# Attention scores in four 64x64 tiles, with the second token tile mirrored

## The reference, cut to what matters

```python
q = _l2norm(q) * q_scale
k = _l2norm(k) * k_scale
sim = jnp.einsum('bhid,bhjd->bhij', q, k) * ATTN_SCALE
dist = -jnp.abs(cols[None, :] - (rows[:, None] + NUM_NULL_KV))
sim = sim + dist[None, None] * slopes[None, :, None, None]
causal_mask = cols[None, :] > rows[:, None] + NUM_NULL_KV
sim = jnp.where(causal_mask[None, None], neg, sim)
attn = jax.nn.softmax(sim, axis=-1)
out = jnp.einsum('bhij,bhjd->bhid', attn, v)
```

## Time and profile before

| | us |
|---|---|
| median of 3 runs | 927.98 (927.37 to 929.27) |
| span of the profiled execution | 927.0 |
| PE busy | 867.1 (94%) |
| DVE busy | 765.1 (83%) |
| ACT busy | 585.8 (63%) |
| POOL busy | 562.4 (61%) |

### The profile page before, as it was taken

How to read it: one execution, slowest core, us unless ns; L and a number is a source line. 1 busy time by engine, 2 the same in 40 slices (tenths; PEclk the granted TensorE clock), 3 DMA queues, 4 the chain that set the end, 5 groups by cost and what they waited for, 6 DMA issues and landing times.

```text
span 927.0 us, 21283 instructions
## 1 busy us (share of the span) xinstructions
PE 867.1 (94%) x8062; PEld 689.6 (74%) x8062; DVE 765.1 (83%) x2457; ACT 585.8 (63%) x1255; POOL 562.4 (61%) x503
## 2 busy tenths in 40 slices
PE   0898899999999999999999999999999999999886
PEld 0685678688777878788787878678787878778676
DVE  6787799889898899889998899888998688865577
ACT  4518773967658672966648673866838774786631
POOL 5227763586638764586746865487644864467723
PEclk9989999999999999999999999999999999999999
DMA  6400000000000000000000000000000000000000
GB/s 165 113 1 0 13 2 2 1 12 2 14 1 0 13 2 13 1 13 1 14 1 1 13 2 14 0 13 2 2 13 1 1 13 2 1 1 1 3 12 12
DMA packets 21991, 11.46 MB, mean 12 GB/s; under 512 B 7552, under 2 KB 21248, under 8 KB 21760
## 3 DMA queue, kind: packets, MB, share of 16 engines
q1 hardware_dynamic: 20032, 9.50, 3.7%
q10 hardware_dynamic: 1856, 0.59, 0.3%
HBM read 7.99 MB, written 2.10 MB: 11 GB/s over the span
## 4 chain that ended last, share of the span: by engine, by line
PE 68%; DVE 16%; ACT 11%; issue 3%; POOL 1%; DMA 0%; SPq 0%; DVEq 0%; ACTq 0%; POOLq 0%
PE bank L1771 9%; PE bank L1772 8%; PE bank L1773 8%; PE bank L1784 5%; PE bank L2029 5%; PE bank L2086 4%; PE bank L1937 4%; PE bank L2035 3%; PE bank L2212 2%; PE bank L2218 2%; PE bank L2101 2%; PE bank L2076 2%; PE bank L2088 2%; PE bank L2187 2%; PE bank L2079 1%
## 5 line engine op out<-in xcount | busy, mean ns | idle before, releaser
L938 POOL TENSOR_TENSOR rnorm<-sumsq,minus_half 128x16 f32<-128x16 f32 x32 | 93.9, 2946 | 55.2 <-DVE sumsq L1574 55.2
L2029 PE MATMUL bank<-qT,kT 64*128 64x256 f32 x512 | 97.3, 387 | 0.0
L944 POOL TENSOR_TENSOR rnorm<-unit,minus_half 128x16 f32<-128x16 f32 x32 | 93.9, 2939 | 4.2 <-DVE unit L1580 4.2
L2035 PE MATMUL bank<-qT,kT 64*128 64x128 f32 x512 | 84.0, 284 | 5.1 <-ACT unit L1208 2.7
L1202 ACT ACTIVATE square<-bank,bias_k,rnorm 128x256 f32<-128x256 f32 x128 | 65.6, 570 | 35.8 <-PE bank L2029 35.8
L2035 PEld LDWEIGHTS bank<-qT,kT 64*128 64x128 f32 x512 | 71.0, 186 | 18.7 <-issue 5.7
L952 POOL TENSOR_SCALAR_AFFINE_SELECT square<-square 128x512 f32<-128x512 f32 x64 | 45.0, 704 | 61.6 <-ACT square L1208 61.5
L1132 ACT ACTIVATE xaT_hi<-bank 128x256 fp32r<-128x256 f32 x16 | 5.9, 382 | 111.1 <-PE bank L1945 110.7
L2029 PEld LDWEIGHTS bank<-qT,kT 64*128 64x128 f32 x512 | 68.7, 186 | 0.2
L2101 PE MATMUL bank<-w_out,qT 128*128 128x128 f32 x512 | 62.8, 276 | 1.2 <-DVE qT L1623 1.2
L1202 ACT ACTIVATE unit<-bank,bias_k,rnorm 128x256 f32<-128x256 f32 x96 | 51.4, 574 | 17.5 <-PE bank L2029 17.5
(11 more groups left out here) (419 smaller groups left out, 2902.7 us busy)
## 6 DMA issues: line engine op xcount, KB each, us to landing
xin<-in_L_attn_x SPq DMA_DIRECT2D x7, 256.0 KB, 2.8
out<-x SPq DMA_DIRECT2D x7, 256.0 KB, 2.3
square<-in_L_attn_w_kv SPq DMA_DIRECT2D x1, 1024.0 KB, 6.5
unit<-in_L_attn_w_q SPq DMA_DIRECT2D x1, 512.0 KB, 5.1
w_out<-in_L_attn_w_out SPq DMA_DIRECT2D x8, 64.0 KB, 2.1
xin<-in_L_attn_x ACTq DMA_DIRECT2D x1, 256.0 KB, 3.1
unit<-in_L_ffn_experts_gate ACTq DMA_DIRECT2D x1, 256.0 KB, 3.4
unit<-in_L_ffn_experts_up SPq DMA_DIRECT2D x1, 256.0 KB, 2.9
```

What stands on the lines that cost most here:

```text
L938: pool.tensor_tensor(rnorm[:, 1, t, :], sumsq[:, t % 2, :], minus_half[:], ALU.pow).then_inc(a_root.sem, 1)
L944: pool.tensor_tensor(rnorm[:, 0, ts, hs], k_sumsq[:, ts, hs], minus_half[:, hs].unsqueeze(1).to_broadcast([P, 2, H // 2]), ALU.pow).then_i ...
L2029: return mm(bank[s][:, 2 * P * i:2 * P * (i + 1)], kT[rs, p, 2 * P * b:2 * P * b + P], qT[rs, p, 2 * P * b:2 * P * (b + 1)], start=True, s ...
L2035: return mm(bank[2][:, 2 * P * s + P * i:2 * P * s + P * (i + 1)], kT[rs, p, ts], qT[rs, p, ts], start=True, stop=True)
```

## The change

Scores come in blocks of 64 keys, in tiles of 64 rows by 64 columns of the array, and each block streams only the queries that can see it: the early tile's first 64 keys 256 queries and its second 64 keys 192, the late tile's blocks 64 and 128. For the latter the late token tile of each sequence is mirrored (token 255 first): `l_x` and `a_nT_` turn odd tiles with a reversed identity. Then, in the late tile, a query sees the keys at its own place and behind it. The mask becomes two selections for each head pair, one for the early diagonal and one for the late with the comparison reversed. The weighted sums read the late queries backwards, so that the output is in token order; for this the matmul over 256 queries is split into two of 128. There are eight signals a unit from the scores instead of three, and the bias of the late keys counts from the other end.

```diff
@@ s_slopes (POOL)
-                for i, start in enumerate((-MID, -(MID + P), -(P - 1), 1)):
-                    made_by(pool.iota(zraw[:, i:i + 1], pattern=[[0, 1]], base=start, channel_multiplier=1, ...
+                for i, (start, step) in enumerate(((-MID, 1), (-(MID + P), 1), (-(P - 1), 1), (P, -1), (P - 1 - MID, -1))):
+                    made_by(pool.iota(zraw[:, i:i + 1], pattern=[[0, 1]], base=start, channel_multiplier=step, ...
@@ mask (POOL)
-                    pd = probs[h % 4][:, 0:4, :]
-                    pool.affine_select(out=pd, in_=pd, compare_op=ALU.is_ge, fill=0.0, base=0,
-                                       pattern=[[0, 4], [1, P]], channel_multiplier=-1).then_inc(a_mask.sem, 1)
-                pool.wait_ge(a_mask.sem, a_mask.at(g, 2 * c + 2))
+                    for step, tile in ((1, 0), (-1, 1)):
+                        pd = probs[h % 4][:, tile:4:2, :]
+                        pool.affine_select(out=pd, in_=pd, compare_op=ALU.is_ge, fill=0.0, base=0,
+                                           pattern=[[0, 2], [step, P]], channel_multiplier=-step).then_inc(a_mask.sem, 1)
+                pool.wait_ge(a_mask.sem, a_mask.at(g, 4 * c + 4))
@@ score_exps (ACT)
-                    act.wait_ge(a_s.sem, a_s.at(g, m + 1))
+                    act.wait_ge(a_s.sem, a_s.at(g, 6 * c + (6 if s else 2)))
...
-                    act.wait_ge(a_s.sem, a_s.at(g, 2 * c + 2))
+                    act.wait_ge(a_s.sem, a_s.at(g, 6 * c + 6))
@@ l_x, a_nT_ (PE)
+            def mirror_odd(dst, ts, src):
+                for t in ts:
+                    last = nc.tensor.transpose(dst[:, t * P:(t + 1) * P], src(t), ident[:, ::-1] if t % 2 else ident[:])
+                return last
@@ a_scores (PE)
-                key1(1, 0)
-                key0(0, 0)
-                key1(1, 1).then_inc(a_odd1.sem, 1)
-                key0(0, 1).then_inc(a_s.sem, 1)
-                key0(1, 0)
-                pe.wait_ge(a_odd1.sem, a_odd1.at(g, c + 1))
-                key1(0, 0)
-                key0(1, 1)
-                key1(0, 1).then_inc(a_s.sem, 1)
+                def early_keys(s, i, k):
+                    rs, cs, (p, b), n = slice(64 * s, 64 * s + 64), slice(64 * k, 64 * k + 64), part(i), 2 * P - 64 * k
+                    return mm(bank[s][cs, 2 * P * (i + 1) - n:2 * P * (i + 1)], kT[rs, p, 2 * P * b + 64 * k:2 * P * b + 64 * k + 64],
+                              qT[rs, p, 2 * P * (b + 1) - n:2 * P * (b + 1)], start=True, stop=True)
+                def late_keys(s, i, k):
+                    rs, cs, (p, b), n = slice(64 * s, 64 * s + 64), slice(64 * k, 64 * k + 64), part(i), 64 * k + 64
+                    tile1 = 2 * P * b + P
+                    return mm(bank[2][cs, 2 * P * s + P * i:2 * P * s + P * i + n], kT[rs, p, tile1 + 64 * k:tile1 + 64 * k + 64],
+                              qT[rs, p, tile1:tile1 + n], start=True, stop=True)
+                late_keys(1, 0, 1)
+                late_keys(1, 0, 0)
+                early_keys(0, 0, 0)
+                early_keys(0, 0, 1)
+                late_keys(1, 1, 0).then_inc(a_odd1.sem, 1)
+                late_keys(1, 1, 1).then_inc(a_odd1.sem, 1)
+                early_keys(1, 0, 0)
+                early_keys(0, 1, 1).then_inc(a_s.sem, 1)
+                early_keys(0, 1, 0).then_inc(a_s.sem, 1)
+                early_keys(1, 0, 1)
+                pe.wait_ge(a_odd1.sem, a_odd1.at(g, 2 * c + 2))
+                late_keys(0, 0, 1)
+                early_keys(1, 1, 0).then_inc(a_s.sem, 1)
+                early_keys(1, 1, 1).then_inc(a_s.sem, 1)
+                late_keys(0, 0, 0)
+                late_keys(0, 1, 1).then_inc(a_s.sem, 1)
+                late_keys(0, 1, 0).then_inc(a_s.sem, 1)
@@ a_mix_ (PE)
-                    last = mm(den[rs, P:2 * P], ones[:], late_sum[c % 2][:, i % 2, j, :], ...
+                    last = mm(den[rs, P:2 * P], ones[:], late_sum[c % 2][:, i % 2, j, ::-1], ...
...
-                        mm(parts[f][rs, :], val[:, 2 * b, h, fs], early(pr, j), start=True, stop=False, ...
+                        mm(parts[f][rs, 0:P], val[:, 2 * b, h, fs], early(pr, j)[:, 0, :], start=True, stop=True, ...
                     for rs, h, pr, j in quad:
-                        last = mm(parts[f][rs, P:2 * P], val[:, 2 * b + 1, h, fs], late(pr, j), start=False, stop=True, ...
+                        mm(parts[f][rs, P:2 * P], val[:, 2 * b, h, fs], early(pr, j)[:, 1, ::-1], start=True, stop=False, ...
+                    for rs, h, pr, j in quad:
+                        last = mm(parts[f][rs, P:2 * P], val[:, 2 * b + 1, h, fs], late(pr, j)[:, ::-1], start=False, stop=True, ...
```

More of the change, by code:

```diff
@@ L469, in program @@
         sel_f = qT[0:LOW + E0, 5, :]
-        zraw = sb("zraw", [P, 4])
+        zraw = sb("zraw", [P, 5])
         x0_loaded = sem("x0_loaded")
@@ L572, in program @@
         a_unit = signal("a_unit", T)
-        a_s = signal("a_s", H)
-        a_odd1 = signal("a_odd1", H // 2)
+        a_s = signal("a_s", 6 * U)
+        a_odd1 = signal("a_odd1", 2 * U)
         a_exp = signal("a_exp", 2 * H)
-        a_mask = signal("a_mask", H)
+        a_mask = signal("a_mask", 2 * H)
         a_late = signal("a_late", U)
@@ L695, in program @@
         POOL_SEL = POOL_IDENT + 7
-        POOL_SLOPE = POOL_SEL + 6 + H
+        POOL_SLOPE = POOL_SEL + 7 + H
         POOL_FILLED = POOL_SLOPE + 8
@@ L857, in s_slopes @@
                 made_by(pool.iota(par_i[:], pattern=[[0, 2]], base=0, channel_multiplier=1))
-                for i, start in enumerate((-MID, -(MID + P), -(P - 1), 1)):
-                    made_by(pool.iota(zraw[:, i:i + 1], pattern=[[0, 1]], base=start, channel_multiplier=1, allow_small_or_imprecise_dtypes=True))
+                for i, (start, step) in enumerate(((-MID, 1), (-(MID + P), 1), (-(P - 1), 1), (P, -1), (P - 1 - MID, -1))):
+                    made_by(pool.iota(zraw[:, i:i + 1], pattern=[[0, 1]], base=start, channel_multiplier=step, allow_small_or_imprecise_dtypes=True))
                 for h in range(H):
@@ L1044, in s_alibi @@
                 for dst, hs, i in ((bias_k0[:, 0:STEEP], slice(0, STEEP), 0), (bias_k0b[:], slice(0, STEEP), 1),
-                                   (bias_k1[:, 0:STEEP], slice(0, STEEP), 0), (bias_k0[:, STEEP:H], slice(STEEP, H), 2),
+                                   (bias_k1[:, 0:STEEP], slice(0, STEEP), 4), (bias_k0[:, STEEP:H], slice(STEEP, H), 2),
                                    (bias_k1[:, STEEP:H], slice(STEEP, H), 3)):
@@ L1946, in half_turn @@
                 return last
+            def mirror_odd(dst, ts, src):
+                for t in ts:
+                    last = nc.tensor.transpose(dst[:, t * P:(t + 1) * P], src(t), ident[:, ::-1] if t % 2 else ident[:])
+                return last
             def l_x(g, h):
                 pe.wait_ge(n_a.steps[h].sem, n_a.steps[h].at(g))
-                half_turn(down_bank(g, h), h, xa).then_inc(l_xt.sem, 1)
+                mirror_odd(down_bank(g, h), tiles(h), lambda t: xa[:, t, :]).then_inc(l_xt.sem, 1)
             def a_null(g):
@@ L2025, in part @@
                     return 2 * (c % 4) + i, seq
[L2027 to L2036, removed]
@@ L2053, in a_nT_ @@
                     pe.wait_ge(l_pick.sem, l_pick.at(g + 1, 1))
-                turn(bank[3], lambda t: null_p[:, t, :, :].rearrange("p i r -> p (i r)")).then_inc(a_nT.sem, 1)
+                mirror_odd(bank[3], range(T), lambda t: null_p[:, t, :, :].rearrange("p i r -> p (i r)")).then_inc(a_nT.sem, 1)
             def a_mix_(g, c):
@@ L2058, in a_mix_ @@
                 quad = [(slice(32 * i, 32 * i + 32), QW * q + i, probs[(2 * c + i % 2) % 4], i // 2) for i in range(QW)]
-                pe.wait_ge(a_mask.sem, a_mask.at(g, 2 * c + 2))
+                pe.wait_ge(a_mask.sem, a_mask.at(g, 4 * c + 4))
                 if c:
@@ L2078, in a_mix_ @@
                 for i, (rs, h, pr, j) in enumerate(quad):
-                    last = mm(den[rs, P:2 * P], ones[:], late_sum[c % 2][:, i % 2, j, :], start=True, stop=True, skip_group_check=True)
+                    last = mm(den[rs, P:2 * P], ones[:], late_sum[c % 2][:, i % 2, j, ::-1], start=True, stop=True, skip_group_check=True)
                 last.then_inc(a_den.sem, 1)
@@ L2085, in a_mix_ @@
                     for rs, h, pr, j in quad:
-                        mm(parts[f][rs, :], val[:, 2 * b, h, fs], early(pr, j), start=True, stop=False, skip_group_check=True)
+                        mm(parts[f][rs, 0:P], val[:, 2 * b, h, fs], early(pr, j)[:, 0, :], start=True, stop=True, skip_group_check=True)
                     for rs, h, pr, j in quad:
-                        last = mm(parts[f][rs, P:2 * P], val[:, 2 * b + 1, h, fs], late(pr, j), start=False, stop=True, skip_group_check=True)
+                        mm(parts[f][rs, P:2 * P], val[:, 2 * b, h, fs], early(pr, j)[:, 1, ::-1], start=True, stop=False, skip_group_check=True)
+                    for rs, h, pr, j in quad:
```

(1 more changed line is left out.)

## The result

| | runs | median us | span of the profiled run |
|---|---|---|---|
| before, same chip | 12 | 928.45 (926.91 to 929.39) | 927.0 |
| after | 12 | 930.02 (928.67 to 930.79) | 928.3 |

The ratio is 1.0018 [1.001, 1.0027]: slower by 1.6 us (by the interval, 0.9 to 2.5), where 1.6 us less was forecast. The range 921 to 931 holds it; the sign is wrong.

A forecast was written before the change was run, and what follows sets the result against it. PE looked full, but ScalarE released 28 of 56 steps between units, with VectorE and POOL waits besides. First group -0.45, five middle -0.6, last but one -0.25, last -0.3: together -1.6 us, 927.98 to 926.4 us; range 921 to 931.

The forecast's parts named there:

- 640 x 2 x 0.83 = 1.07 us, 0.21 us less per unit: Scores on PE: 640 columns instead of 768 for each 64x64 tile, 0.21 us less per unit of four heads.
- when the first exp may start: ScalarE's first exp after a unit's scores: comes 0.05 us sooner through a shorter weight-load lead.
- nothing left: Rival: signals or later first exps undo the 0.05 us gained at the first exp; 927.9 us, chance 0.13.
- The offsets of the middle group: Shifts of each unit's scores start in a middle group: -0.2 at unit 4, ending 0.12 us earlier; five groups -0.6.
- then ScalarE paces: Middle groups after scores 4: ScalarE's exps release the next scores, giving -0.25 at scores 5 and -0.3 at scores 6.
- +0.18 lands on PE: Second half of `den` (L2079), units 5 and 6 of middle groups: two selects delay PE by 0.18 us, no slack.
- PE has 0.76 us to spare in each unit: Last attention group: PE idles 0.76 us per unit, so slower selects cost nothing except after the last scores.
- First group -0.45, last but one -0.25: Group sums: first -0.45 us (more PE-bound steps, `l_down` ahead of sums), last but one -0.25 us (scores 7 pass on 0.2).
- Sums +0.01, backward reads 0, signals 0: Split weighted sums cost +0.01 us per unit; reading operands backwards and eight signals instead of three cost 0.
- (b): Rival: the scores' saving passes wherever ScalarE does not release the step; -6.1 us, 921.9 us, chance 0.17.
- (c): Rival: POOL becomes the pace, half a select costing nearly a whole one; about +6 us, 934 us, chance 0.14.
- (e): Rival: scores' column tiles run serially, not side by side; +0.85 us a unit, about 970 us, chance 0.06.

The follow-up runs named there:

- e3: The changed kernel with `l_c` padded with zero rows from 40 to all 128 rows: 928.29 us, ratio to before 0.9998.
- e5: The changed kernel with one 128x512 select per head pair, leaving out the late tile's mirrored mask: 928.45 us, ratio to before 1.0001.
- e6: The changed kernel with both the padded `l_c` of e3 and the single select of e5: 925.98 us, ratio to before 0.9968.
- e1: The kernel before with scores cut into 64x64 tiles, all query columns kept, signals as after, no mirror, one select: 930.38 us, ratio to before 1.0021.
- e9: e7 with the late keys' wait for `a_odd1` moved behind one more matmul: 924.80 us, ratio to before 0.9959.
- e10: e7 with the late keys' wait for `a_odd1` moved behind two more matmuls: 924.94 us, ratio to before 0.9965.
- e2: The kernel before with two selects of 128x256 for each head pair, nothing else: 930.08 us, ratio to before 1.0021.
- e11: The changed kernel with each select waiting only for its own exps, `l_c` as it was: 927.63 us, ratio to before 0.9994.
- e7: e3 with each select waiting only for its own exps, nothing left out: 924.92 us, ratio to before 0.9964.
- e4: The kernel before with `l_c` padded to 128 rows, the control for e3: 929.34 us, ratio to before 1.0009.

## Why the prediction was wrong

Two steps failed: the unchanged `l_c` was priced at nothing, and the second select was priced only behind units 5 and 6 of the middle groups and behind the last scores of the run. The sum by group shows where (change against before, us, from the profiles; the middle groups are five together):

| | forecast | after | e3, layout's cost out | e5, POOL's out | e6, both out |
|---|---|---|---|---|---|
| first | -0.45 | +0.88 | +0.68 | +0.27 | +0.02 |
| middle | -0.60 | +0.42 | -0.50 | -0.35 | -1.43 |
| last but one | -0.25 | +0.62 | +0.33 | +0.23 | -0.08 |
| last with tail | -0.30 | +0.03 | +0.03 | -0.33 | -0.33 |

Taking out either cost alone brings the kernel only back to before (e3 and e5 in the table of runs). Step by step, as it was put:

- **"640 x 2 x 0.83 = 1.07 us, 0.21 us less per unit"** failed in size: 0.14. The columns alone gave less still: e1 has the same tiles with all 768 columns and took 1.46, after 1.37 with 640. What stands around the columns is open (e9, e10).
- **"when the first exp may start", 0.05 sooner**: right (1.173 to 1.126 us). The two more signals ahead of the first exp did not undo it, so the rival "nothing left" did not happen in this way.
- **The offsets of the middle group** failed from unit 5 on; this is the layout's part. The prediction carried -0.2 to -0.3 through units 4 to 6, since "then ScalarE paces". Start of each unit's scores in a middle group, after less before, counted from unit 0's:

| unit | 1 | 2 | 3 | 4 | 5 | 6 | 7 | next 0 |
|---|---|---|---|---|---|---|---|---|
| forecast | | | | -0.2 | -0.25 | -0.3 | -0.1 | -0.12 |
| measured | -0.13 | -0.26 | -0.12 | -0.22 | +0.09 | +0.01 | +0.53 | +0.11 |

  Up to unit 4 it holds. Then `l_c` stands before the scores of units 5, 6 and 7, and the switch between its layout and the scores' costs PE more than the scores save. Behind unit 6's scores it costs them again: scores and `l_c` took 1.80 us to the sums before and take 1.79 after (557.39 to 559.18). PE, not ScalarE, now ends those waits: the last exp to the next scores was 0.05 us and is 0.40, 0.11 and 0.61. I priced the instructions that the change adds and removes, and not what the unchanged neighbour shared with the old ones; the earlier trace rows begins 0.13 us behind an `l_c` that I left out. With that cost out (e3), a middle group is 0.10 us shorter, against the 0.12 forecast, and the reason given for it, the POOL release of unit 6's sums, is the one that the trace of e3 shows. That the numbers are so close is in part luck: scores 5 and 6 start at -0.13 and -0.20 there, not at -0.25 and -0.3, and the pair of selects was 0.05 cheaper than forecast.
- **"+0.18 lands on PE" at L2079**: right where it was put, size 0.13. It failed in the places where I put nothing: its weight over the run was 1.6 us by e2 and by e5. In the first group I had counted on `l_down` ahead of the sums; there, and in the last but one, PE now waits for `late_sum` where it had not (after; in e6 the first of these two waits is 0.11 us):

```profile
147.76 0.43 PE L2094 MATMUL bank<-mixed,ones 128*32 128x128 f32 x8 [0.54 <-POOL mixed L962]
756.62 0.42 PE L2094 MATMUL bank<-mixed,ones 128*32 128x128 f32 x8 [0.27 <-POOL mixed L962]
```

  In the last group "PE has 0.76 us to spare in each unit" was read from one unit. The selects of unit 1 queue up there behind a longer POOL step, and the four of them then run in a row in 1.49 us, where before the two took 1.22 (850.22 to 851.44):

```profile
851.62 1.49 POOL L952 TENSOR_SCALAR_AFFINE_SELECT square<-square 128x256 f32<-128x256 f32 x4
854.50 0.43 PE L2094 MATMUL bank<-mixed,ones 128*32 128x128 f32 x8 [0.92 <-POOL mixed L962]
```

  PE's idle time at L2094 was 0.64 us here before and is 0.92, with another 0.38 ahead of the first half of `den`. Its sums end late, and unit 3's scores start 0.32 us after the last exp instead of 0.05. In e5 it is 0.05 again and the group ends at -0.33.
- **First group -0.45, last but one -0.25** failed beyond these costs: with both out (e6) they are +0.02 and -0.08, so the columns saved there gave almost nothing. What takes them was not followed.
- **Sums +0.01, backward reads 0, signals 0**: the first two as forecast (from the second half of `den` to the next line ahead of unit 6's scores, 1.63 us before and 1.64 after; 273 ns). No run changes the signals alone; e1 has as many more as after, and its first exp comes 1.17 us behind the scores, as before.
- **Rivals**: (b) needs the saving to pass; even with both causes out (e6) it is 2.4 of the 6.1 us. (c) had the right engine but the wrong price (0.77 a pair, not 1.2). (e) did not happen: e1 streams 768 columns a row half in each of two column tiles, and its scores are no slower, so the four tiles do run side by side.

## What to carry to other kernels

When a step gets another tile shape, price its neighbours too: read how soon the matmul ahead of it and the one behind it overlap with it now, because the overlap of `l_c` with the scores was seen here between equal layouts only, and losing it cost about as much over the run (1.9 us by e1, which changes only the scores' tiles and signals) as the whole change is worth without its costs (2.4 by e6). A cheap mend, where the overlap is lost anyway, is to bring the small neighbour into the layout of what stands on its other side, even by padding it with zeros (1.7 us by e3, 2.7 by e11 against e7); where the overlap is still there, the same padding cost some 0.9 (e4). When a mask is split, give each half the wait of its own inputs: the split then shortens the tail instead of lengthening it. And a release read in two units is not a list of all the places that have no slack.

## What was not expected of the hardware

- Behind a 40-row matmul streaming 512 columns, a 64-row matmul that also uses 128 columns of the array started as soon as 0.01 us later, and one of another layout never before 0.42 (22 places, after). In e3 the same 512 columns on 128 rows, behind their own layout, let 64*64 scores start 0.32 us later, and a matmul of their own layout starts 0.23 behind such a one (560.10 to 560.33). The price is not simply one for each side: before, `l_c` behind unit 6's scores had their layout and the sums still started 0.43 us behind it (558.28 to 558.71).
- The weight load behind the `a_odd1` wait started 0.79 us after the first scores wherever in the order the wait stood (e7, e9, e10), 0.14 us behind the end of the matmul that it waits for (0.65, an end that the profile models).
- Two selects in a row take 0.77 us, less than the 0.82 of two fixed parts; a 128x256 alone takes 0.41.
